# First layer of a four-layer graph network on one core: the order of its tile visits, where the second product begins, and where counts and code chains run

## The reference

```python
terms = [x, L @ x]
for _ in range(2, K):                       # K = 4
    terms.append(2.0 * (L @ terms[-1]) - terms[-2])
return jnp.einsum('kni,kio->no', jnp.stack(terms, axis=0), weight)
# x = layernorm(x + that)
```

```python
rank = jnp.cumsum(mask, axis=1)             # layer 2
pos = rank - (deg - k)
w = mask * jnp.where(pos > 0, DECAY ** (k - pos), 0.0)
```

## The kernel before

| part | visits | products | also |
|---|---|---|---|
| A | quarters 0, 1, 2 (24) | one each, pass 0 | base, row block 0 |
| B | quarter 3 (8) | pass 0, and pass 1 of quarter 3 in six | base, counts (3), row blocks 0 to 3 |
| C | quarter 2 (8) and the two kept tiles of quarter 3 | pass 1 | chain (2), row block 1 |
| D | quarter 1 (8) | pass 1 | counts (1), rows |
| E | quarter 0 (8) | pass 1, and pass 2 of quarter 0 in six | counts (0), chain (0), rows |
| F | two kept tiles of quarter 0, quarter 1 (8) | pass 2 | chain (1) |
| G | quarter 2 (8) | pass 2 | counts (2), row blocks 2, 3 |
| H | quarter 3 (8) | pass 2 | chain (3) |

## Time and profile before

### The profile page before, as it was taken

One profiled execution on the slowest core, in us unless ns is written; L12 is line 12 of the kernel. 1 busy time (PEld: TensorE's weight loads), 2 busy tenths in 40 slices (PEclk: granted clock), 3 DMA queues, 4 the chain that ended last, 5 costly groups with the idle time before them and its releaser, 6 DMA issues. The chain is left out here.

```text
span 1482.8 us, 18446 instructions
## 1 busy us (share of the span) xinstructions
PE 1333.8 (90%) x6874; PEld 592.7 (40%) x6874; DVE 1202.6 (81%) x1560; ACT 983.8 (66%) x919; POOL 222.0 (15%) x150
## 2 busy tenths in 40 slices
PE   6999899999989899899999999989988888888893
PEld 1333234333334344454454454534423434333342
DVE  5999988994856797877977977568597899899997
ACT  0002352884484586567667667786689899999985
POOL 1000000000000000000000001142134445444550
PEclk9999999999999899999999999999979999999995
DMA  9999869988999656554444452244633656556610
GB/s 360 409 409 409 313 227 412 411 329 309 403 411 412 261 198 211 181 179 172 171 168 163 167 181 100 71 132 139 227 108 119 202 168 218 175 175 213 214 57 29
DMA packets 134560, 341.56 MB, mean 230 GB/s; under 512 B 7876, under 2 KB 57480, under 8 KB 134280
## 3 DMA queue, kind: packets, MB, share of 16 engines
q1 hardware_dynamic: 118240, 320.88, 59.3%
q10 hardware_dynamic: 16232, 19.51, 3.9%
HBM read 321.49 MB, written 17.83 MB: 229 GB/s over the span
## 5 line engine op out<-in xcount | busy, mean ns | idle before, releaser
L1087 PE MATMUL ps<-ring,X 128*64 128x512 f32 x512 | 236.1, 610 | 13.7 <-DVE ring L2439 8.4
L1088 PE MATMUL ps<-work,X 128*64 128x512 f32 x512 | 236.2, 610 | 0.0
L843 POOL TENSOR_TENSOR ring<-ring,work 128x1024 f32<-128x1024 f32 x72 | 170.1, 2362 | 223.6 <-DVE work L2831 223.6
L1683 ACT ACTIVATE work<-ring 128x2048 f32<-128x2048 f32 x64 | 122.4, 1913 | 81.6 <-PE ps L1103 36.2
L950 PE MATMUL ps<-ring,work 128*64 128x512 f32 x704 | 164.7, 617 | 9.0 <-DVE Y L2093 5.9
L820 POOL TENSOR_SCALAR work<-ring 128x1024 int16<-128x1024 uint8 x24 | 26.8, 1120 | 971.3 <-DMA ring<-codes 899.0
L2439 DVE TENSOR_SCALAR ring<-ring 128x2048 f32<-128x2048 f32 x64 | 78.3, 1224 | 66.6 <-ACT work L1683 66.2
L1087 PEld LDWEIGHTS ps<-ring,X 128*64 128x64 f32 x512 | 67.5, 140 | 151.7 <-issue 141.8
L2123 DVE TENSOR_TENSOR work<-work,ring 128x1024 f32<-128x1024 f32 (+1 forms) x98 | 107.9, 1101 | 9.3 <-DMA ring<-in_adjT 7.6
L1510 ACT ACTIVATE work<-ring 128x4096 bf16<-128x4096 f32 x23 | 82.9, 3615 | 43.1 <-PE ps L899 43.0
L1432 ACT ACTIVATE turn_in<-ps 128x512 f32<-128x512 f32 x12 | 7.2, 596 | 150.3 <-PE ps L950 149.4
(11 more groups left out here) (387 smaller groups left out, 2702.8 us busy)
## 6 DMA issues: line engine op xcount, KB each, us to landing
ring<-in_adjT SPq DMA_DIRECT2D x86, 2048.0 KB, 13.9
work<-in_adjT SPq DMA_DIRECT2D x26, 2048.0 KB, 22.9
ring<-in_adjT SPq DMA_DIRECT2D x24, 1024.0 KB, 9.1
ring<-in_adjT SPq DMA_DIRECT2D x48, 512.0 KB, 4.0
ring<-codes SPq DMA_DIRECT2D x32, 512.0 KB, 4.0
ring<-in_adjT SPq DMA_DIRECT2D x64, 256.0 KB, 3.2
codes<-work ACTq DMA_DIRECT2D x32, 256.0 KB, 6.4
codes<-work ACTq DMA_DIRECT2D x64, 128.0 KB, 2.9
```

What stands on the lines that cost most here:

```text
L843: nc.gpsimd.tensor_tensor(u.edges[:, cols], u.edges[:, cols], u.angle[:, cols], ALU.mult).then_inc(weighted, 1)
L1087: nc.tensor.matmul(ps[0:F, h, :], rows, ring[:, r, 2 * (m % 2) + i, cols], start=start, stop=stop)
L1088: mm = nc.tensor.matmul(ps[F:P, h, :], rows, negs[:, m % 2, i, cols], start=start, stop=stop)
L1683: nc.scalar.activation(negs[:, pair], ring[:, r, 2 * pair:2 * pair + 2, :], ACT.Relu, scale=-1.0).then_inc(negs_made, 1)
```

## The change

Layer 0 has a new list of visits: 80 visits, 76 loads, still 96 products.

| part | visits | products | also |
|---|---|---|---|
| A | quarters 0, 1 (16) | pass 0 | base, row block 0 |
| A2 | quarter 2 in the order 4, 5, 0, 1, 2, 3, 6, 7 | pass 0, and pass 1 of quarter 2 for tiles 0 to 3 (turn EARLY, banks 6 and 7) | base, counts (2), all row blocks in the four double visits, block 0 in the others |
| B | quarter 3 (8) | pass 0, and pass 1 of quarter 3 in six | base, counts (3), all row blocks in the double visits |
| C | quarter 2, tiles 4 to 7 and the two kept tiles of quarter 3 | pass 1 | rows |
| D | quarter 1 (8) | pass 1 | counts (1), rows |
| E | quarter 0 (8) | pass 1, and pass 2 in six | counts (0), chain (0), rows |
| F | two kept tiles of quarter 0, quarter 1 (8) | pass 2 | chain (1) |
| G | quarter 2 (8) | pass 2 | chain (2), row block 3 of tiles 4 to 7 |
| H | quarter 3 (8) | pass 2 | chain (3) |

The half sum of turn EARLY is copied by ACT to a place in T2's room (`parked`), and DVE adds it when it copies turn 4. Banks, waits and the places of small steps follow. From visit 17 to 47 DVE reads turned products and counts at the start of a visit, ahead of its masks and row adds. In part B the base product of a visit is issued one visit later on PE, and some counts are issued between the two products of the next visit. The preparation of weights is split and moved into part B, `first` starts at the third visit of part C. The slots follow from the same planner; with the new list `slot_after` is [76, 79, 77, 74], where it was [80, 79, 81, 82] for the last visits 76 to 79 and 80 to 83.

```diff
+        parked = T2_words[:, QC:2 * QC]
...
-        TURN_QUARTERS = (0, 1, 2, 3, 3, 2, 1, 0, 0, 1, 2, 3)
-        TURN_BANKS = (0, 4, 0, 4, 0, 6, 4, 0, 6, 4, 0, 4)
-        COUNT_QUARTERS = (3, 1, 0, 2)
+        TURN_QUARTERS = (0, 1, 2, 3, 2, 3, 1, 0, 0, 1, 2, 3)
+        EARLY = 3 * NQ
+        TURN_BANKS = (0, 4, 0, 6, 4, 2, 6, 4, 2, 6, 4, 6, 6)
+        BASE_BANKS = (2, 6, 2, 4)
+        COUNT_QUARTERS, COUNT_BANKS = (2, 3, 1, 0), (4, 0, 0, 0)
+        BASES_READ = (2, 4, 7, 9)
...
+        visits = [Visit(q, g, (q,), base=(q, g), rows=(0,)) for q in range(2) for g in range(NS)]
+        A2_AT = len(visits)
+        for s, g in enumerate((4, 5, 0, 1, 2, 3, 6, 7)):
+            visits.append(Visit(2, g, (2, EARLY) if g < 4 else (2,), base=(2, s), counts=(0, s),
+                                rows=(0, 1, 2, 3) if g < 4 else (0,)))
         B_AT = len(visits)
         for s, g in enumerate((6, 0, 1, 2, 3, 4, 5, 7)):
-            visits.append(Visit(3, g, (0, 1) if g < 6 else (0,), base=(3, s), counts=(0, s), rows=(0, 1, 2, 3)))
+            visits.append(Visit(3, g, (3, 5) if g < 6 else (3,), base=(3, s), counts=(1, s),
+                                rows=(0, 1, 2, 3) if g < 6 else (0,)))
         C_AT = len(visits)
-        visits += [Visit(2, g, (1,), chain=(0, g), rows=(1,)) for g in range(NS)]
-        visits[C_AT + 2:C_AT + 2] = [Visit(3, 6, (1,)), Visit(3, 7, (1,))]
+        visits += [Visit(2, g, (4,), rows=(1, 2)) for g in range(4, NS)]
+        visits += [Visit(3, g, (5,), rows=(1, 2, 3)) for g in range(6, NS)]
...
-        visits += [Visit(2, g, (2,), counts=(3, g), rows=(2, 3)) for g in range(NS)]
+        visits += [Visit(2, g, (10,), chain=(2, g), rows=() if g < 4 else (3,)) for g in range(NS)]
...
+            def park_product():
+
+                act.wait_ge(tile_multiplied, turn_ends[EARLY])
+                bank = TURN_BANKS[EARLY]
+                nc.scalar.activation(parked, ps[:, bank:bank + 2, :].rearrange("p h c -> p (h c)"), ACT.Copy).then_inc(
+                    base_read, 1)
...
-                if m in (0, 3) and a.sign_n:
+                if m < 2 and a.sign_n:
                     act.wait_ge(counts_made, a.sign_n)
-                if m and a.sign_n == NS:
+                if a.sign_n == 2 * NS:
                     act.wait_ge(based, SLOTS)
                     act.wait_ge(first_read, 9)
...
             for a in visits:
                 if a.t == F_AT:
                     read_turned(7)
+                if a.t - 1 in TURNS_AT and A2_AT < a.t < E_AT + 2:
+                    read_turned(TURNS_AT.index(a.t - 1))
+                if a.t - 1 in COUNT_TURN_AT and a.t < E_AT + 2:
+                    read_counts(COUNT_TURN_AT.index(a.t - 1))
                 waits_for_tile(dve, a)
                 if a.base:
                     make_masks(a)
```

More of the change, by code:

```diff
@@ L534, in adjacency_stack, with __init__ @@
         LAST_TURN = 3 * NQ - 1
-        TURN_QUARTERS = (0, 1, 2, 3, 3, 2, 1, 0, 0, 1, 2, 3)
-        TURN_BANKS = (0, 4, 0, 4, 0, 6, 4, 0, 6, 4, 0, 4)
-        COUNT_QUARTERS = (3, 1, 0, 2)
+        TURN_QUARTERS = (0, 1, 2, 3, 2, 3, 1, 0, 0, 1, 2, 3)
[4 more added lines that the diff above has]
+        BASES_READ = (2, 4, 7, 9)
         class Visit:
-            def __init__(self, q, g, passes, base=None, counts=None, chain=None, rows=()):
-                self.q, self.g, self.passes = q, g, passes
+            def __init__(self, q, g, turns, base=None, counts=None, chain=None, rows=()):
+                self.q, self.g, self.turns = q, g, turns
@@ L554, in adjacency_stack @@
+        visits += [Visit(3, g, (5,), rows=(1, 2, 3)) for g in range(6, NS)]
         D_AT = len(visits)
-        visits += [Visit(1, g, (1,), counts=(1, g), rows=(1, 2, 3)) for g in range(NS)]
+        visits += [Visit(1, g, (6,), counts=(2, g), rows=(1, 2, 3)) for g in range(NS)]
         E_AT = len(visits)
-        visits += [Visit(0, g, (1,) if g < 2 else (1, 2), counts=(2, g), chain=(1, g), rows=(1, 2, 3)) for g in range(NS)]
+        visits += [Visit(0, g, (7,) if g < 2 else (7, 8), counts=(3, g), chain=(0, g), rows=(1, 2, 3)) for g in range(NS)]
@@ L558, in adjacency_stack @@
         F_AT = len(visits)
-        visits += [Visit(0, 0, (2,)), Visit(0, 1, (2,))]
-        visits += [Visit(1, g, (2,), chain=(2, g)) for g in range(NS)]
+        visits += [Visit(0, g, (8,)) for g in range(2)]
+        visits += [Visit(1, g, (9,), chain=(1, g)) for g in range(NS)]
         G_AT = len(visits)
-        visits += [Visit(2, g, (2,), counts=(3, g), rows=(2, 3)) for g in range(NS)]
+        visits += [Visit(2, g, (10,), chain=(2, g), rows=() if g < 4 else (3,)) for g in range(NS)]
@@ L563, in adjacency_stack @@
         H_AT = len(visits)
-        visits += [Visit(3, g, (2,), chain=(3, g)) for g in range(NS)]
-        for v in visits[E_AT:F_AT]:
-            v.late_count = True
+        visits += [Visit(3, g, (11,), chain=(3, g)) for g in range(NS)]
+        for a in visits:
+            a.counts_between, a.counts_last, a.bases_last = [], [], []
+        for a, b in zip(visits, visits[1:]):
+            if a.base:
+                (b if B_AT <= visits.index(a) < C_AT - 1 else a).bases_last.append(a)
+            if a.counts:
+                m, s = a.counts
+                if m == 3 and s < NS - 1 or m == 1 and s == 0 or m == 0 and s == 1:
+                    b.counts_between.append(a)
+                elif m == 0 and s == 0:
+                    b.counts_last.append(a)
+                else:
+                    a.counts_last.append(a)
@@ L614, in adjacency_stack @@
                 a.sign_n = signed_n
-                a.sign_half = signed_n % 2 if 0 < a.counts[0] < 3 else 1
+                a.sign_half = signed_n % 2 if a.counts[0] > 1 else 1
                 signed_n += 1
@@ L965, in _ @@
                     turn_counts(COUNT_TURN_AT.index(a.t))
-                if a.late_count and a.counts[1]:
-                    count(visits[a.t - 1])
-                if len(a.passes) == 2:
+                for b in a.counts_between:
+                    count(b)
+                if len(a.turns) == 2:
                     multiply(a, 1)
[L970 to L973, removed]
+                for b in a.bases_last:
+                    add_base(b)
+                for b in a.counts_last:
+                    count(b)
                 if a.t == F_AT - 1:
@@ L1471, in read_base @@
             def read_base(q):
-                bank = 2 + 4 * (q % 2)
+                bank = BASE_BANKS[q]
                 act.wait_ge(based, (q + 1) * NS)
```

123 lines of the change are left out of this document (71 added, 52 removed).

## The result

| | kernel before | changed kernel |
|---|---|---|
| median of 20 runs, us | 1485.46 | 1491.35 |
| ratio, with 95% interval | | 1.0037 (1.0021 to 1.0052) |
| the profiled execution, us | 1484.56 | 1493.84 |
| first product of part F | 365.93 | 360.54 |
| last product of layer 0 starts | 485.02 | 483.78 |

The changed kernel is slower by 0.37%, some 5.5 us, within half a percent. The forecast was 1489.0, 4.4 us slower, with 0.66 on no change.

A forecast was written before the change was run, and what follows sets the result against it. Loads bound the kernel first, then PE until part F, then loads to layer 0's last tile, then PE in layer 1. Terms -8.1 + 4.6 + 7.9 = +4.4 us on 1484.56 gave 1489.0; 8-in-10 range 1479 to 1494.5.

The forecast's parts named there:

- no change: Whole kernel: a time between 1477.3 and 1492.1 us, about 0.5% either way, counts as the same; chance 0.66.
- Part 1: Visit 16 to the start of part F: 18.9 us gone, 10.8 added, so part F begins 8.1 us earlier.
- The waits that were to go: Before part F: waits for T1, a bank, counts, masks and turn 2's copy, with slow steps behind; 18.9 us in all.
- the mask wait of visit 17: Visit 17: DVE reads turn 1 before making masks, so PE waits 1.2 to 1.4 us.
- the start of part D: First sign waits for all of `first`: PE waits 2.0 us, plus 1.2 taken for a possible slow product (0 to 2.4).
- the slower rival: Part C: DVE reaches visit 38 late by three rows (3.65 us), first sign late, slow product; 1494.2 us, chance 0.18.
- Part 2: Part F to the last tile: eight more stores in part G, where the DMA is full, add 4.6 us.
- the upper bound: Part G's eight stores: bounds 0 if they slip in between, 4.6 us as in part H; 4.6 taken.
- Part 3: Hand-over to layer 1: first load issued only after the last product, so DVE starts 7.9 us later (bounds 4 to 8.5).
- The sum: Whole kernel: -8.1 + 4.6 + 7.9 = +4.4 us on 1484.56, giving 1489.0.
- What the four loads bought: Parts C and D: no visit waits for a tile, so the four loads taken out buy nothing there.

The follow-up runs named there:

- experiment 1: Changed kernel with its six slots given other places, so the last visit's tile lies away from layer 1's first loads; ratio to the kernel before 0.9983.
- experiment 6: Changed kernel with slots' places mended and part G's code stores cut to 16 of 128 partitions, rest filled in part E; ratio to the kernel before 0.9954.
- experiment 2: Kernel before with the places of slots 1 and 4 traded, so layer 1's first tile takes the very last visit's place; ratio to the kernel before 1.0053.
- Experiment 3: Changed kernel with DVE's fourth read of `first` moved ahead of the row adds of visit 38; ratio to the kernel before 1.0022.
- experiment 4: Kernel before, old list with 80 loads, with DVE's reads of turned products and counts ahead of masks, chain and rows; ratio to the kernel before 0.9944.
- the whole change with all its mends: Changed kernel with slots' places mended, fourth read of `first` ahead of rows, turn 1's read behind visit 17's masks again; ratio to the kernel before 0.9949.

## Why the prediction was right, point by point

The result lies 2.4 us from the forecast, on its side, and each term has its row in the trace after.

- **Part 1.** Forecast -8.1 us to part F's start, measured 360.54 - 365.93 = -5.4 in the profiled execution. The waits that were to go went, and the mask wait of visit 17 was 1.41 for a forecast of 1.2 to 1.4. The term that this execution shows larger is the start of part D, priced at 3.2 us: it is the wait of 2.92, the slow product (6.14 against 3.65) and the slow count (1.04 against 0.62), 5.8 us. Two things went into it. The wait was 0.9 us longer than counted, because DVE's third read of `first` (257.09) stood ahead of the copy (257.70). And the product came out slow, which the forecast had priced at the middle between slow and not. That part is chance: experiments 1 and 6 have the same order and the same wait without a slow product, and there the step costs 2.7 and 2.9 us and part F begins at 359.00 and 357.51, 6.9 and 8.4 us before 365.93. The kernel before has such a spread too: experiment 2, with its order of visits, begins part F at 364.35. DVE and ACT in the changed kernel:

```profile
257.09 0.69 DVE L2107 TENSOR_TENSOR Y<-ps,Y 128x512 f32<-128x512 f32 x1
257.70 0.68 DVE L2135 COPY turn_in<-ps 128x512 f32<-128x512 f32 x1
258.30 3.74 DVE L2175 TENSOR_TENSOR work<-work,ring 128x1024 f32<-128x1024 f32 x3
261.95 0.68 DVE L2105 TENSOR_TENSOR Y<-Y,X 128x512 f32<-128x512 f32 x1
262.67 0.69 DVE L2107 TENSOR_TENSOR Y<-ps,Y 128x512 f32<-128x512 f32 x1
```

```profile
263.53 3.62 ACT L1549 ACTIVATE work<-ring 128x4096 bf16<-128x4096 f32 x1 [6.10 <-DVE Y L2107]
```

  Experiment 3 takes this step away and part F moves by 5.9 us against the changed kernel's trace, which has the slow product, but by 2.9 against experiment 6, which has not. This was also the place of the slower rival, which wanted DVE about 2 us late; it was half that.
- **Part 2.** Forecast +4.6 us for eight stores, measured 123.2 - 119.1 = +4.1 in the changed kernel and 4.7 by experiment 6. Tiles in part G came 5.7 to 6.1 us apart, where 5.7 was forecast. Taking the upper bound was right: the DMA was full with the stores (414 GB/s) as without them (409), so they take time from the loads.
- **Part 3.** Forecast +7.9 us, measured 20.4 - 12.2 = +8.2 from the last product's start to layer 1's first (504.17 - 483.78 against 497.19 - 485.02), and 8.0 and 7.9 by the ratios of experiments 1 and 2 (8.6 and 8.7 by their traces). It took 8.8 us from issue to DVE, near the 8.5 of the earlier trace rows. The Trainium skill (DMA: Bandwidth & Descriptors, Anatomy of one DMA) gives an estimate of 6.8 us for such a load; the trace is 2.0 us above it.
- **The sum** of the three is +7.0 us at layer 1's first product. The profiled execution ended 9.3 us later than before, the medians lie 5.9 apart and the ratio says 5.5. The other 2.3 us of the profiled pair are behind layer 0 (987.9 against 985.6 us), where the code is the same and executions differ by more than that (experiment 3); the medians carry less of it. The forecast's own sum was 2.6 us under the measured 7.0, nearly all of it the start of part D. With the fast product of experiment 6 the three terms would be some +4, near the forecast's 4.4, and the medians' 5.5 to 5.9 lie between. So the mechanism and the sizes held, but that the number came within 2.4 us is partly luck: slow products alone move part F by up to 3 us between executions, and the interval of the ratio is 2.3 us to each side.
- **What the four loads bought.** Nothing that shows, as forecast: no tile is late in parts C to E with 76 loads, nor with 80 in experiment 4. By experiment 4 the gain is in the reads ahead of the masks (the new list without them was not run); the new list moved stores into a full stretch, made the last tile's room layer 1's first, and put a sign behind a chain of reads.

## What to carry to other kernels

Where a ring of rooms passes from one stage to the next, look up which room is used last and which is loaded first: the same room in both roles emptied the DMA queue here and cost 8 us, nearly the whole 8.8 from a load's issue to its use, and renaming the rooms mended it for nothing. Count the bytes moved into a stretch where the DMA is full, stores too, and don't expect a gain from loads saved in a stretch where the queue isn't the bound. When one change reorders work and also moves the reads, try the cheap part alone first; here it gave as much as the whole change with all its mends. And before a slow product is counted as the price of a wait, look whether another execution with the same wait has it.

## What the runs showed of the hardware

A load of 2 MB into an empty queue, with two more right behind it, had its tile in use 8.8 us after the issue (489.17 to 497.99), and 9.3 in experiment 2 (488.64 to 497.95). A byte code's store of 0.26 MB cost 0.6 to 0.7 us of a full queue (4.7 us for seven eighths of eight stores; tiles 5.70 against 5.12 us apart in the earlier trace rows). A wait of PE of 2.0 to 2.9 us was sometimes followed by a slow product (6.14 us at a granted clock of 0.59 behind 2.92; 5.35 at 0.68 behind 2.07) and sometimes not (3.65 at 1.00 behind 2.93 in experiment 6, and behind 2.02 in experiment 4), and one slow product had no wait at all ahead of it (5.35 at 0.68 in experiment 1, at 240.01). I had not expected that the time behind layer 0, of equal code, would go from 982.3 (experiment 6) to 996.3 us (experiment 3) over the profiled executions, more than any of the three terms of the sum.
